# Selective-scan mixer between two channel-mix layers: order of ScalarE's decays, the gated product, the output quarters and the turned delta u

## The reference

```python
x = x + 0.5 * ffn(layernorm(x))
x = x + mixer(layernorm(x))
x = x + 0.5 * ffn(layernorm(x))

# mixer, with 1024 channels and 16 states a channel
xz = (inp - mean(inp)) @ W_in
x, z = split(xz)
x = silu(depthwise_conv(x, 4 taps, padding (1, 2)) + conv_b)
B, C = split(x @ W_x)
delta = softplus(x @ W_dt + b_dt)
h[t] = exp(delta[t] * A) * h[t-1] + delta[t] * B[t] * x[t]
y[t] = sum over states of h[t] * C[t]
out = ((y + x * D) * silu(z)) @ W_out + inp
```

## Time and profile before

| what | value |
|---|---|
| median of 3 runs | 5207.4 us |
| the profiled execution, its own time | 5209.97 us |
| its span, first to last instruction | 5208.0 us |
| mean granted TensorE clock | 0.987 |
| PE busy | 4916.9 us, 94% |
| DVE busy | 4510.7 us, 87% |
| ACT busy | 3849.1 us, 74% |
| POOL busy | 3756.8 us, 72% |

### The profile page before, as it was taken

The page is one execution under the profiler, slowest core; times in us unless marked ns, Lnnn a source line. Parts: engine busy times, 40 slices in busy tenths (PEclk is TensorE's granted clock), DMA queues, the critical chain, the costliest instruction groups (busy, mean ns, idle before and its releaser), DMA issues. The chain is left out here.

```text
span 5208.0 us, 83685 instructions
## 1 busy us (share of the span) xinstructions
PE 4916.9 (94%) x25472; PEld 3971.2 (76%) x25472; DVE 4510.7 (87%) x7540; ACT 3849.1 (74%) x9976; POOL 3756.8 (72%) x1701
## 2 busy tenths in 40 slices
PE   8999989999999999999999999999999999979999
PEld 6777767777777777777777777777777777768887
DVE  6777669999999999999999999999899999977775
ACT  5556558888888888888888888888888888854443
POOL 1111059999999999999999999999999999931110
PEclk9999999999999999999999999999999999989999
DMA  3222231111111111111111111111111111211111
GB/s 83 91 80 81 102 110 46 46 46 48 58 53 55 46 46 46 46 46 46 46 51 54 46 46 54 58 54 50 46 46 46 46 46 46 66 58 53 65 57 41
DMA packets 154802, 292.21 MB, mean 56 GB/s; under 512 B 40688, under 2 KB 58096, under 8 KB 154352
## 3 DMA queue, kind: packets, MB, share of 16 engines
q1 hardware_dynamic: 154352, 286.82, 16.6%
HBM read 218.60 MB, written 68.18 MB: 55 GB/s over the span
## 5 line engine op out<-in xcount | busy, mean ns | idle before, releaser
L1009 POOL TENSOR_TENSOR mx_dbu<-mx_bs,mx_du 128x2048 f32<-128x2048 f32 (+2 forms) x513 | 2047.3, 3991 | 291.7 <-DVE mx_hp L1350 287.4
L1167 ACT ACTIVATE mx_ps_da<-mx_dl,mx_a 128x256 f32<-128x256 f32 x3584 | 1558.6, 466 | 72.9 <-DVE mx_hp L1350 39.9
L1350 DVE TENSOR_TENSOR_SCAN mx_hp<-mx_ps_da,mx_hst,mx_dbu 128x256 f32<-128x256 f32 x1792 | 1333.5, 744 | 215.3 <-ACT mx_ps_da L1167 213.6
L1027 POOL TENSOR_TENSOR mx_hp<-mx_hp,mx_cs 128x1024 f32<-128x1024 f32 (+1 forms) x576 | 1220.7, 2125 | 4.6 <-ACT mx_hst L1176 4.6
L1472 PE MATMUL mx_ps_m<-mx_u,mx_w_dt 128*128 128x256 f32 x4096 | 947.9, 385 | 93.6 <-ACT mx_duT L1148 67.8
L1350 DVE TENSOR_TENSOR_SCAN mx_ps_da<-mx_ps_da,mx_hst,mx_dbu 128x256 f32<-128x256 f32 x1344 | 937.9, 748 | 4.8 <-ACT mx_ps_da L1167 1.8
L1472 PEld LDWEIGHTS mx_ps_m<-mx_u,mx_w_dt 128*128 128x128 f32 x4096 | 759.6, 190 | 239.0 <-issue 136.2
L1363 DVE TENSOR_TENSOR mx_hc<-mx_ps_da,mx_cs 128x512 f32<-128x512 f32 x1024 | 696.0, 680 | 10.3 <-PE mx_ps_y L1502 8.3
L1502 PEld LDWEIGHTS mx_ps_y<-mx_ident,mx_hp 128*128 128x128 f32 x4096 | 511.0, 142 | 203.6 <-issue 114.8
L1502 PE MATMUL mx_ps_y<-mx_ident,mx_hp 128*128 128x128 f32 x4096 | 620.3, 274 | 8.4 <-POOL mx_hp L1027 8.4
L1502 PE MATMUL mx_ps_y<-mx_ident,mx_hc 128*128 128x128 f32 x4096 | 617.2, 273 | 4.1 <-DVE mx_gy L1330 3.9
(11 more groups left out here) (134 smaller groups left out, 8349.3 us busy)
## 6 DMA issues: line engine op xcount, KB each, us to landing
mx_bs<-bc_scratch SPq DMA_DIRECT2D x128, 512.0 KB, 4.6
mx_cs<-bc_scratch SPq DMA_DIRECT2D x128, 512.0 KB, 3.7
mx_hT<-hT_scratch SPq DMA_DIRECT2D x32, 518.0 KB, 4.2
hT_scratch<-f_h2T SPq DMA_DIRECT2D x16, 1024.0 KB, 8.9
mx_xo<-xs_scratch SPq DMA_DIRECT2D x32, 512.0 KB, 3.7
x_scratch<-mx_xo SPq DMA_DIRECT2D x32, 512.0 KB, 2.9
f_x<-in_L_attn_inp SPq DMA_DIRECT2D x12, 1024.0 KB, 6.5
xs_scratch<-f_x SPq DMA_DIRECT2D x12, 1024.0 KB, 4.3
```

Source lines behind the costliest of these rows:

```text
L1009: G.tensor_tensor(dbu[:, n % NM:n % NM + k].rearrange("p n s t -> p (n s) t")[:, skip:, :], bs[:, g:g + k].rearrange("p n s t -> p (n s) t ...
L1027: G.tensor_tensor(h, h, cs[:, g:g + k, SD:SG, :], ALU.mult).then_inc(s_pr, k - 1 + step_to(n))
L1167: ins = A.activation(dst[:, k, :], dl[:, b % NL, :], ACT.Exp, scale=a_sb[:, b, s:s + 1])
L1350: ins = V.tensor_tensor_scan(bank if in_psum(p) else hp[:, n % NH, k, :], da, db, 0.0 if first else hst[:, b, SG * g + s:SG * g + s + 1], ...
```

## The change

The diff does this:

- In an `on_pe` unit ACT no longer goes through the place for the first half (its decay is made earlier); the second pair's keep and decay come first, and what was due at the first half (in these units the relu) follows them.
- The silu visit moves from the end of ACT's unit to the place ahead of copy_z and clear.
- DVE's gated product moves between the two pairs' scans.
- `BC_AT` goes from unit 22 to 23 of the chunk before; with it the clear from 21 to 22 and the copy from 24 to 25.
- Output parts: units 26, 30, 2, 10, 13, 14, 15, 18 become 26, 30, 2, 8, 10, 14, 17, 19. The first copy out and the second residual go from unit 12 to 9.
- `turn_du` moves in PE's unit from the front to the place between the two sums.

```diff
--- before.py
+++ after.py
@@ -792,7 +792,7 @@
 
         IN_AT = [NG * b - NU - 9 for b in range(ND)]
         GATE_AT = [NG * b - 11 for b in range(ND)]
-        BC_AT, CLEAR = [-10], -1
+        BC_AT, CLEAR = [-9], -1
         DU_AT = [NG * b - 2 for b in range(ND)]
         SB = ND // 2
         DT_AT = [NG * b - 8 for b in range(ND)]
@@ -801,11 +801,11 @@
         YT_AT = [NG * b + NG + 5 for b in range(ND)]
         BACK_AT = [NG * b + NG + 5 for b in range(ND)]
         YG_AT = [NG * b + NG + 6 for b in range(ND)]
-        OUT_AT = [NU - 6, NU - 2, NU + 2, NU + 10, NU + 13, NU + 14, NU + 15, NU + 18]
+        OUT_AT = [NU - 6, NU - 2, NU + 2, NU + 8, NU + 10, NU + 14, NU + 17, NU + 19]
         OUT_PARTS = len(OUT_AT) // TJ
         LAST_OUT_AT = [24, 26]
-        RES_AT = [NU - 7, NU + 12]
-        EVAC_AT = [NU + 12, NU + 20]
+        RES_AT = [NU - 7, NU + 9]
+        EVAC_AT = [NU + 9, NU + 20]
         TAPS, ZCOPY, COPY = 1, 1, 2
         RELU, EXP, LOG, ADD = 2, 2, 3, 5
         KEEP_LAG, SUMC_LAG, SUM_LAG = 1, 3, 4
@@ -1247,14 +1247,14 @@
                     for half in range(2):
                         p = 2 * n + half
                         if on_pe(p):
-                            pass
+                            continue
                         elif in_psum(before(p)):
                             keep_psum(i, p)
                             decay(i, p)
                         else:
                             bank_scanned(i, p)
                             decay(i, p)
-                        if half == 0:
+                        if half == 0 or on_pe(p - 1):
                             for bb, s in due(DT_AT, n, i, RELU):
                                 relu(i + s, bb)
                             for bb, s in due(IN_AT, n, i, TAPS):
@@ -1270,6 +1270,13 @@
                         keep(i, n - KEEP_LAG)
                     elif not is0(i):
                         keep(i - 1, NU + n - KEEP_LAG)
+                    if due(Z_SILU_AT, n, i):
+                        A.preload_act_table_set("silu_and_others")
+                        for k, s in due(Z_SILU_AT, n, i):
+                            silu_z(i + s, (par + s) % 2, k)
+                        for k, s in due(U_SILU_AT, n, i):
+                            silu_u(i + s, (par + s) % 2, k)
+                        A.preload_act_table_set("natural_log_exp_and_others")
                     for bb, s in due(GATE_AT, n, i, ZCOPY):
                         copy_z(i + s, (par + s) % 2, bb)
                     for bb, s in due(BC_AT, n, i, CLEAR):
@@ -1287,13 +1294,6 @@
                         log(i + s, bb)
                     for bb, s in due(DIAG_AT, n, i):
                         b_diagonals(i + s)
-                    if due(Z_SILU_AT, n, i):
-                        A.preload_act_table_set("silu_and_others")
-                        for k, s in due(Z_SILU_AT, n, i):
-                            silu_z(i + s, (par + s) % 2, k)
-                        for k, s in due(U_SILU_AT, n, i):
-                            silu_u(i + s, (par + s) % 2, k)
-                        A.preload_act_table_set("natural_log_exp_and_others")
 
             def epilogue():
                 for n in range(NU):
@@ -1406,12 +1406,12 @@
                     if n - 1 in ALL_IN_PSUM:
                         times_c_second(i, n - 1)
                     scan(i, n, 0, 1, first)
+                    finish(i, par, n)
                     scan(i, n, 1, 0, first)
                     taps(i, par, n, 1)
                     times_c(i, n)
                     taps(i, par, n, 2)
                     scan(i, n, 1, 1, first)
-                    finish(i, par, n)
                     taps(i, par, n, 3)
 
             def epilogue():
@@ -1582,8 +1582,6 @@
                         k = LAST_OUT_AT.index(n)
                         for j in range(TJ):
                             last_out_product(j, range(2 * k, 2 * k + 2))
-                    for b, s in due(DU_TURN_AT, n, i):
-                        turn_du(i + s, b)
                     for b, s in due(DBU_AT, n, i):
                         b_times_du(i + s, b)
                     for part, s in due(OUT_AT, n, i):
@@ -1603,6 +1601,8 @@
                         sum_states(i, n - SUM_LAG)
                     elif not is0(i):
                         sum_states(i - 1, NU + n - SUM_LAG)
+                    for b, s in due(DU_TURN_AT, n, i):
+                        turn_du(i + s, b)
                     if n >= SUMC_LAG:
                         sum_psum_states(i, n - SUMC_LAG)
                     elif not is0(i):
```

## The result

The changed kernel takes **5281.5 us** (median of 4 runs, 5274.2 to 5282.8) against 5207.2; the ratio is 1.014, 95% interval 1.0122 to 1.0158. It is slower, as forecast, but by 74 us where 22 were forecast, and just above the range given (5280). The profiled execution is the quickest of the four, 5274.24 us with a span of 5272.4 and a granted clock of 0.980; the other three, at 0.978, took 5281.4 to 5282.8 and have no trace.

What follows compares the result with a forecast made beforehand. PE (94% busy) and DVE (87%) leave only idle time on their shared chain to win. Terms -0.65 + 0.3 + 1.1 = +0.75 us per chunk, +23 over 30 chunks, +22 after end corrections: 5229 us, range 5165 to 5280.

Steps and rivals of the forecast that it cites:

- the clock behind the stand: At the B and C product: clock falls in 3 of 4 chunks, costing 1.5 us each, 1.1 per chunk.
- the gain that is left: At unit 24's second pair: of the 3.0 us DVE is early after the second visit, 0.65 per chunk remain.
- The first visit: Unit 6: second pair's decay first lets DVE go on 0.73 us earlier; moved quarter hidden at unit 8; gain 0.7.
- Unit 16: Two fewer output quarters ahead of its tap on PE remove DVE's 2.14 us wait, leaving DVE 2.87 early.
- The stand: PE idle 2.9 us before the B and C product, waiting for ACT's clear behind the second silu visit.
- the rival in which the gain of the second visit goes through (B): Clear comes early enough, product doesn't delay unit 24's tap; 2.6 us per chunk gained, 5127 us; chance 0.07.
- bounds of 0 and 2.3: Range of clock cost per chunk, unit 6 and B and C product together: no fall, or both in each chunk.
- The gated product: On DVE between the pairs: fills idle time, may wait about 1 us in unit 18, swallowed by the next tap.
- Unit 6's fall: Behind PE's stand there, shrunk to 2.1 us: fall chance 2 in 5, 0.8 us counts, 0.3 per chunk average.
- Rival C: Slower still: clock falls at both places in nearly each chunk, +1.75 us per chunk, 5260 us; chance 0.17.
- my worse reading: By the skill's rule the clock falls in each chunk, making the sum about 0.4 us per chunk worse.

Runs made afterwards that it cites:

- the filled stand: Changed kernel with two f32 products (1.7 us, results thrown away) at the start of PE's unit 23, the clear waiting for them: 5248.8 us.
- the clear first: Changed kernel with the clear moved to unit 21 ahead of the silu visit, B and C product left at unit 23: 5196.7 us.
- The last kernel: Kernel before with moved output quarters (third at unit 6), plus ACT's order and gated product changed in units 6 and 22 alone: 5121.0 us.

## Why the prediction was right or wrong

The direction and the place of the loss were right, the size wasn't: in the sum of -0.65 + 0.3 + 1.1 us a chunk two terms were mis-sized, the clock behind the stand and the gain that is left.

- **The first visit** held: the wait in unit 6 fell to 1.58 us, unit 7's first decay holds DVE up (0.2), and the quarter at unit 8 doesn't show.
- **Unit 16** held: its wait is gone, and alone the quarters give 31 us.
- **The stand** held to 0.1: 3.0 us against 2.9, ended by the clear, and the changed place alone costs 67 us. The rival in which the gain of the second visit goes through (B) is refuted by the row of L1461 itself.
- **The clock behind the stand** was mis-sized most. Forecast: a fall in 3 of 4 chunks, 1.5 us each, 1.1 a chunk. Measured: 21 of 22, 15 that cost about 1.5 (L1461 at 4.98 to 5.33 against 3.64) and 6 that cost 2.9 (6.58), (15 x 1.5 + 6 x 2.9) / 22 = 1.8 a chunk. I took the cost of a fall from the place behind a stand of 2.5 us, where a slow input product took 3.43 us; I had no row for a longer product behind a longer stand. The forecast's bounds of 0 and 2.3 allow at most 1.5 for this place, and that was too narrow.
- **The gated product** was the cost that I put at nothing, beyond a wait in unit 18 that the next tap would swallow. It is why of 3.0 us hardly 0.1 was left, and not 0.65. It waits 0.23 in unit 10 and 1.02 in unit 18 in the mean, and DVE's idle time in unit 0 grew from 0.2 to 0.5. An estimate from the rows: take what L1461 lasts beyond 3.64 us off each chunk, and look at those without a fall in unit 6. They come to 121.8 us in the mean in the changed kernel and to 121.3 with the gated product put back, and such chunks of the kernel before lasted 122.0. So without this edit 0.7 a chunk is left, as forecast (0.65), and the edit takes some 0.5 of it. Put back, it gave 36 us, more than 0.5 a chunk makes; the rest comes through the clock (no product of 6.5 us any more). Through which of its waits the 0.5 comes isn't shown.
- **Unit 6's fall** came out at the size forecast by two errors that cancel: 5 of 22 in place of 2 in 5, and 1.1 us each in place of 0.8, which makes 0.26 against 0.3.
- The sum by what was measured, -0.1 + 0.3 + 1.8 = 2.0, fits the 1.96 us a chunk between 123.91 and 121.95. Over 31 chunks the two profiled executions differ by 63 us, the stretch before them is 2.6 shorter and that behind the last 3.8 longer, which makes the 64.
- Rival C (both falls in nearly each chunk, 5260) was nearest in time, and even that was short. It had the clock right at one place alone: 21 of 22 at the product, but 5 of 22 in unit 6. By its own terms it is -0.65 + 2.3 = 1.65 a chunk and not 1.75, and the chances of the rivals add up to 0.29 for faster and 0.57 for slower, not 0.28 and 0.58; neither slip matters.
- The Trainium skill (TensorE: Matmul & The Clock Gate, Part 1) states that the throttled state is the default and that activity releases it. A fall in each chunk was my worse reading of that. The trace is near that reading at the product, 21 of 22, and not in unit 6, 5 of 22.

## What to carry to other kernels

A step that is moved past a long visit on a third engine must be costed with what now stands behind its semaphore: one `clear` of 0.36 us behind a 4.6 us visit, and the product that waits for it, cost 67 to 89 us in all. On TensorE price each stand that a change makes longer twice, once for itself and once for the work behind it at half clock. Where the stand can't be avoided, put work that is due anyway into it: one output quarter in the stand of unit 6 gave 14 us, all of it clock. An order that helps where an engine comes late should be made there alone. And when a change gains less than its waits say, compare the chunks in which the clock kept up with the others: here the gain was there in the first and gone in the second.

## What was not expected of the hardware

- After one and the same stand of 3.00 us the next product took 3.64, about 5.2 or 6.58 us, and the granted clock over 7 us was 1.00, 0.77 or 0.54. The clock can stay down for nearly the whole of a 6.58 us product even though TensorE is at work.
- How often the clock falls isn't set by the length of a stand alone. With 2.36 us in unit 6 it fell there in 5 of 22 chunks in the changed kernel (chunks of 123.9 us), 9 with the product back at unit 22 (121.1) and 20 with the filled stand (123.0). With 1.9 to 2.0 us in unit 0 it fell in 9 of 22 (ACT's order and the gated product), 12 (the B and C part undone) and 17 (the clear first). Stands of up to 1.78 us in unit 0 never had a fall behind them, and 1.80 to 2.08 behind the second visit had none either; but one of 1.45 to 1.52 in unit 7, close behind one of 1.15, had it in 12 of 22 (the turn alone). What sets it beside the length stays open.
- One kernel can scatter by 46 us: 5168.6 to 5214.6 over ten runs of the one with the clear first, at a granted clock of 0.988 in the quickest and 0.978 in the slowest. Falls alone don't make it so, since the one with the quarters alone has them in half of its chunks and stayed within 4 us (5174.6 to 5177.9). The last kernel, without falls in the 22 chunks of its trace, also stayed within 4 us in four runs (5119.4 to 5122.6).
